# Order of ScalarE, VectorE and TensorE work inside a step: x's halves, weight splits, the spread and the division

## The chip, the cores and the metric

The kernel runs on one core of a Trainium2 chip. The metric is the device time of one execution in microseconds (us), the median of several runs. Lower is better. All arithmetic that matters for the error is float32: most products are made of three matmuls on "upper" and "lower" halves of each operand (a number rounded to fp32r, and what is left of it), so every operand needs two passes over it ahead of TensorE: one on ScalarE, which rounds (`..._upper`, `..._hi`), and one on DVE (VectorE), which subtracts (`..._lower`, `..._lo`).

## What is computed

Two layers of attention plus a mixture of experts on 4096 tokens of 512 numbers, cut here to its frame:

```python
x = L0_attn_x                                   # (2, 2048, 512)
xn = _layernorm(x)
s = _L0_attn_ref(xn, Wq, Wkv, Wk, Wv, Wo)       # 16 heads, window of 128 keys + 16 persistent ones
g = silu(_L0_ffn_ref(xn, ...))                  # 32 experts, 6 per token, and a shared one
x = x + s * g
xn = _layernorm(x)
s = _L1_attn_ref(xn, W_in, ...)                 # Y = (A * Q) @ W_out + X, A summed over the sequence
g = silu(_L1_ffn_ref(xn, router_weight, ...))
x = x + s * g
```

In the first attention each query tile sees its own 128 keys, the 128 before it, and the 16 persistent ones; softmax, times the values, then `Wo`.

## The kernel before, in words

The program is five phases, one after the other: `phase_front` (norm, projections, with the routing inside the next), `phase_attend` (first attention, L602), `phase_experts` (L1083), `phase_mix` (the combining stage, L1410) and `phase_last` (L2077). Each phase has one instruction stream for each engine, written out by hand and run in that order; semaphores tie the streams together. Nothing is reordered by a scheduler, so the order of the calls in a step is the order on the engine. An engine whose next instruction waits holds everything behind it.

**The attention stage** walks over 512 (tile, head) pairs in steps `s`, 16 a tile, 32 tiles. What each engine does in a step is a few calls. TensorE: `score(s + 3)` (L867, needs that DVE has read the score bank of three steps ago), `turn(s)` in odd steps (four transposes of a pair of heads' probabilities, L884), `values(u, g)` in every fourth (L897), in step 17 of a tile (`X_AT`) `turn_sums` (L907), then `spread` (L925: the inverse row sums of the tile, spread over the 32 columns of each head, out of `a_xT`) and `pers_values` (L913: the persistent keys' share, the last that is added to `a_psO`). DVE: `top(s + 3)` (L1027: mask, scale and row maximum), `copy_out` of transposed pairs (L1038), `divide` (L1051: `a_o` = `a_psO` times `a_rb`) and `out_lo`. ScalarE: `exps(s + 2)` (L972), `sums_out` (L988: writes `a_xT`), `inverse_out` (L994: writes `a_rb`), `out_hi` (L1000). `values(u + 1, 0)` overwrites `a_psO` and so waits for `divide(u)`.

**The combining stage** walks over 8 groups of 512 tokens, 18 steps `k` a group, with a shared expert of layer 0 in 6 blocks of three steps: gate product, up product, down product of the block before. `q` counts blocks. Next to it, the finished group is combined: `sums` (L1910, DVE: four additions out of `b_psY`), `gates` (L1787, ScalarE: four Silu), `residual` (L1918, L1920, L1922, DVE: three passes for each of four tiles), then the norm, and for each of its four tiles TensorE's `turn` (L1676, transposes into `c_psX`), `x_upper` (L1804, ScalarE) and `x_lower` (L1961, DVE), `router` (small matmuls into `c_psX`, waits for `x_lower`), and two products `keys(t, 0)` and `keys(t, 1)` into the one bank `c_psK`, which DVE empties after each (L1973). Those four tiles start at 8, 12, 16 and 20 steps behind the start of the group that follows, so the fourth falls into step 2 of the group after that, where the next group's `sums` and `gates` stand as well. The weights of block `q + 2` are split in the third step of each block: `gu_upper` (L1763, ScalarE) and `gu_lower` (L1883, DVE, waits for `gu_upper`). TensorE needs them four steps later.

In group 0 the stage also folds the norm's gamma and beta into layer 1's weights (`fold`, `fold_out`, `fold_upper`).

Of the kernel before, what the change touches and what calls it, by code (L numbers as in the profile page):

```python
# [601 lines left out]
def phase_attend(nc, env):  # L602
# [23 lines left out]
    with ctx:  # L626
# [137 lines left out]
        X_AT = 17  # L764
# [87 lines left out]
        def _(pe):  # L852
# [88 lines left out]
            for s in STEPS:  # L941
                if s + SR < N:
                    score(s + SR)
                if s < N:
                    turn(s)
                for g in range(NGR):
                    if (u := tile_of(s, GH * g + GH - 1 + LAG)) is not None:
                        values(u, g)
                if (u := tile_of(s, X_AT)) is not None:
                    turn_sums(u)  # L950
                if (u := tile_of(s, X_AT + 2)) is not None:
                    spread(u)
                if (u := tile_of(s, X_AT + 3)) is not None:
                    pers_values(u)
                for c in range(KC):
                    if (u := tile_of(s, X_AT + 8 + c)) is not None:
                        project(u, c)
# [59 lines left out]
        def _(dve):  # L1017
# [50 lines left out]
            for s in STEPS:  # L1068
                if s + SR < N:
                    top(s + SR)  # L1070
                if (u := tile_of(s, X_AT - 3)) is not None:
                    invert(u)
                if s < N:
                    copy_out(s)
                if (u := tile_of(s, X_AT + 4)) is not None:
                    divide(u)
                if (u := tile_of(s, X_AT + 5)) is not None:
                    out_lo(u)
                if (u := tile_of(s, X_AT + 12)) is not None:
                    finish(u)  # L1080
# [329 lines left out]
def phase_mix(nc, env):  # L1410
# [14 lines left out]
    with ctx:  # L1425
# [331 lines left out]
        def _(act):  # L1757
# [78 lines left out]
            for g, k, after in steps():  # L1836
                if g is not None:
# [8 lines left out]
                    elif q + 2 < QS:  # L1846
                        gu_upper(q + 2)
# [7 lines left out]
                for n, rel in after:  # L1855
# [12 lines left out]
                    if (t := tile_at(n, rel, XS)) is not None:  # L1868
                        x_upper(t)
                    if (t := tile_at(n, rel, XS + 4)) is not None:  # L1870
                        squares(t)
                    if rel == 25:
                        act.wait_ge(nn_ready, n + 1)
                        act.activation(rn[n % 2][:, :], nn[n % 2][:, :], ACT.Sqrt).then_inc(nroot_ready, 1)

        @block.vector
        def _(dve):
# [155 lines left out]
            for g, k, after in steps():  # L2033
                if g is not None:
# [6 lines left out]
                    elif k % 3 == 2:  # L2041
                        h_lower(q)
                        if q + 2 < QS:
                            gu_lower(q + 2)
                if g == 0:
                    fold(k)
                for n, rel in after:
# [11 lines left out]
                    if (t := tile_at(n, rel, XS)) is not None:  # L2059
                        x_lower(t)  # L2060
# [11 lines left out]
                    if rel == A_AT + 1:  # L2072
                        dve.wait_ge(a_full, n + 1)
                        dve.tensor_copy(env.aparts[:, n, :], psA).then_inc(a_used, 1)

# [549 lines left out]
```

## Time and profile before

| | us |
|---|---|
| median of 3 runs (lowest, highest) | 4580.51 (4570.82, 4585.73) |
| the profiled execution: time, span | 4576.1, 4574.2 |
| attention stage, 385 to 952: length, PE busy, DVE busy, ACT busy | 567, 496, 369, 385 |
| combining stage, 2460 to 3246: length, PE busy, DVE busy, ACT busy | 786, 729, 371, 249 |
| TensorE waits in the attention stage for `a_xT` (27 times) | 18.9 |
| TensorE waits in the attention stage for `a_o` (25 times) | 17.4 |
| TensorE waits in the combining stage for x's lower half (18 times) | 26.8 |
| TensorE waits once for the fold's first sum | 7.4 |

The first column names a thing, the second gives it in us of the one profiled execution (but for the median). TensorE (PE) is the busiest engine in both stages, at 87% and 93% of them.

### The profile page before, as it was taken

The numbers are of one execution on the slowest core, as the hardware profiler recorded it, in microseconds if no ns is written. First come the engines' busy times: TensorE is split into PE (matmuls) and PEld (weight loads), VectorE is DVE, ScalarE is ACT, GpSimd is POOL, SyncE is SP. The second block draws the span as 40 slices with busy tenths as digits, with TensorE's granted clock in tenths as the row PEclk, the third lists the DMA queues.
The fourth block names the chain that finished last, engine by engine and source line by source line (L and its number), as shares of the span: only waits on it lengthen the run. The fifth ranks groups of instructions, "written<-read, shape, count | busy, mean of one in ns | idle before, by whom it ended". The sixth has DMA issues, their size and how long they took to land. (4 is left out here: it accounts for less than half of the span.)

```text
span 4574.2 us, 68643 instructions
## 1 busy us (share of the span) xinstructions
PE 4213.9 (92%) x23045; PEld 3557.8 (78%) x23046; DVE 2097.7 (46%) x4006; ACT 1663.7 (36%) x3234; POOL 1220.5 (27%) x1809
## 2 busy tenths in 40 slices
PE   6966888879999999999997999998799999999998
PEld 5854667668989888888886777776578888788887
DVE  4457666644444444444444554453333333333333
ACT  2214766643343434343332333332222222222222
POOL 0012444434444444444442233333100000000000
PEclk8877999989999999999998999998899999999999
DMA  5776666635555556565554443342423222221221
GB/s 199 284 231 162 128 136 128 114 96 118 113 126 120 130 112 130 114 131 118 124 116 130 168 150 121 133 134 71 143 76 104 97 87 75 97 99 63 97 81 48
DMA packets 351750, 560.87 MB, mean 123 GB/s; under 512 B 33057, under 2 KB 198593, under 8 KB 347330
## 3 DMA queue, kind: packets, MB, share of 16 engines
q1 hardware_dynamic: 282770, 394.19, 29.3%
q0 software_dynamic: 68784, 164.10, 16.9%
q8 instruction: 120, 1.97, 0.2%
q14 instruction: 76, 0.62, 0.1%
HBM read 383.84 MB, written 174.34 MB: 122 GB/s over the span
## 5 line engine op out<-in xcount | busy, mean ns | idle before, releaser
L1206 POOL DMA_INDIRECT acc_d<-e_yw,e_to x208 | 336.1, 1616 | 342.4 <-ACT e_yw L1339 330.6
L2244 POOL DMA_DIRECT2D out<-d_res x32 | 17.3, 542 | 1305.3 <-DVE d_res L2476 1305.3
L2423 DVE TENSOR_TENSOR d_h<-d_sg,d_psU 128x512 f32<-128x512 f32 x144 | 99.1, 688 | 520.1 <-PE d_psU L107 461.7
L972 ACT ACTIVATE a_pr<-a_sm,a_nmax 128x272 f32<-128x272 f32 x512 | 264.0, 516 | 164.3 <-DVE a_nmax L1027 122.5
L105 PE MATMUL e_psG<-e_gu,e_xT 128*128 128x352 f32 x832 | 286.3, 344 | 8.5 <-DVE e_xT L1393 8.5
L1401 DVE TENSOR_TENSOR e_h<-e_sg,e_psU 128x352 f32<-128x352 f32 x208 | 108.4, 521 | 387.3 <-ACT e_sg L1352 383.9
L1027 DVE CUSTOM_DVE_ANT_0 a_sm<-a_psS,a_mask 128x272 f32<-128x272 f32 x512 | 213.1, 432 | 156.7 <-PE a_psS L867 134.8
L107 PE MATMUL e_psU<-e_gu,e_xT 128*128 128x352 f32 x832 | 268.8, 323 | 0.0
L105 PE MATMUL e_psU<-e_gu,e_xT 128*128 128x352 f32 x832 | 268.5, 323 | 0.0
L106 PE MATMUL e_psU<-e_gu,e_xT 128*128 128x352 f32 x832 | 268.3, 323 | 0.0
L106 PE MATMUL e_psG<-e_gu,e_xT 128*128 128x352 f32 x832 | 267.8, 322 | 0.0
L107 PE MATMUL e_psG<-e_gu,e_xT 128*128 128x352 f32 x832 | 267.8, 322 | 0.0
L105 PE MATMUL e_psY<-e_wd,e_hT 128*128 128x512 f32 (+1 forms) x624 | 264.0, 423 | 1.2 <-DVE e_hT L1384 1.2
L2351 ACT ACTIVATE d_hT<-d_h 128x512 fp32r<-128x512 f32 x144 | 91.0, 632 | 459.0 <-DVE d_h L2423 401.0
L1187 POOL DMA_INDIRECT e_xg<-xn_d,e_idx x208 | 208.4, 1002 | 177.1 <-POOL e_idx L1184 166.3
L1352 ACT ACTIVATE e_sg<-e_psG 128x352 f32<-128x352 f32 x208 | 96.8, 465 | 425.7 <-PE e_psU L107 424.7
L107 PE MATMUL e_psY<-e_wd,e_hT 128*128 128x512 f32 (+1 forms) x624 | 248.0, 397 | 0.0
L106 PE MATMUL e_psY<-e_wd,e_hT 128*128 128x512 f32 (+1 forms) x624 | 247.5, 397 | 0.0
L2345 ACT ACTIVATE d_sg<-d_psG 128x512 f32<-128x512 f32 x144 | 86.0, 598 | 422.9 <-PE d_psG L107 422.7
L1333 ACT ACTIVATE e_hT<-e_psH 128x384 fp32r<-128x384 f32 x208 | 102.7, 494 | 372.8 <-PE e_psY L107 200.0
L105 PE MATMUL d_psG<-d_x,d_gu 128*128 128x512 f32 x576 | 225.1, 391 | 12.9 <-DMA d_x<-xT_d 12.7
L105 PE MATMUL d_psU<-d_x,d_gu 128*128 128x512 f32 x576 | 227.5, 395 | 0.0
(423 smaller groups left out, 11901.8 us busy)
## 6 DMA issues: line engine op xcount, KB each, us to landing
d_gu_raw<-in_wgu SPq DMA_DIRECT2D x144, 512.0 KB, 3.2
qk_d<-f_qk SPq DMA_DIRECT2D x32, 1024.0 KB
a_q<-qk_d SPq DMA_DIRECT2D x96, 256.0 KB
a_k<-qk_d SPq DMA_DIRECT2D x96, 256.0 KB
e_rawgu<-in_w_gate SPq DMA_DIRECT2D x32, 704.0 KB
e_rawgu<-in_w_up SPq DMA_DIRECT2D x32, 704.0 KB
b_gu_raw<-in_wgu SPq DMA_DIRECT2D x40, 512.0 KB, 3.9
xT_d<-f_xT SPq DMA_DIRECT2D x16, 1024.0 KB
```

The costliest lines, as they stand in the source:

```text
L105: pe.matmul(out, lhs[0], rhs[1], start=first, stop=False, **kw)
L106: pe.matmul(out, lhs[1], rhs[0], start=False, stop=False, **kw)
L107: return pe.matmul(out, lhs[0], rhs[0], start=False, stop=last, **kw)
L972: act.activation(pr[half][:, h % HH, :], sm[s % SR][:, :], ACT.Exp, bias=nmax[s % SR][:, :], scale=-1.0, accum_out=rs[u % 2][:, h:h + 1]). ...
L1027: dve.tensor_tensor_reduce(out=sm[s % SR][:, :], in0=psS[s % SR][:, PERSIST:2 * KW], in1=m[:, :], scale=-SCALE, scalar=3.0e38, op0=ALU.add ...
L1187: pool.indirect_dma_start(xg[:, :], None, env.xn_d, bass.IndirectOffsetOnAxis(ap=idx[:, :].bitcast(U32), axis=0))\
L1206: pool.indirect_dma_start(env.acc_d, bass.IndirectOffsetOnAxis(ap=to[:, :].bitcast(U32), axis=0), yw[:, :], None, compute_op=ALU.add).then ...
L1333: act.activation(hT[0][:, :, :], psH[:, :, :], ACT.Copy).then_inc(hT_hi, 1)
L1352: act.activation(sg[:, :], psG[:, 0:M], ACT.Silu).then_inc(sg_ready, 1)
L1401: dve.tensor_tensor(hv[:, :], sg[:, :], psU[:, 0:M], ALU.mult).then_inc(h_ready, 1)
L2351: act.activation(h2[q % 2][0][:, :], hv[q % 2][:, :], ACT.Copy).then_inc(h_hi, 1)
L2423: ins = dve.tensor_tensor(hv[q % 2][:, :], sg[q % 2][:, :], psU[:, :], ALU.mult)
```

## The change

Four places are touched, two in each stage; no instruction is added or removed on any engine.

- TensorE, attention: `spread(u)` goes from the end of step 19 to step 20, behind that step's score and ahead of `values(u, 3)`.
- DVE, attention: `divide(u)` goes to the front of its step 21, ahead of `top` and `copy_out`.
- ScalarE and DVE, combining: `x_upper` and `x_lower` go ahead of the combining work of the step (and of the fold).
- ScalarE and DVE, combining: `gu_upper` and `gu_lower` go to the end of the step, behind the combining work (and the fold).

```diff
@@ phase_attend, tensor @@
+                if (u := tile_of(s, X_AT + 3)) is not None:
+                    spread(u)
                 for g in range(NGR):
...
-                if (u := tile_of(s, X_AT + 2)) is not None:
-                    spread(u)
@@ phase_attend, vector @@
             for s in STEPS:
+
+                if (u := tile_of(s, X_AT + 4)) is not None:
+                    divide(u)
                 if s + SR < N:
                     top(s + SR)
...
-                if (u := tile_of(s, X_AT + 4)) is not None:
-                    divide(u)
@@ phase_mix, scalar @@
-                    elif q + 2 < QS:
-                        gu_upper(q + 2)
+
+                for n, rel in after:
+                    if (t := tile_at(n, rel, XS)) is not None:
+                        x_upper(t)
...
-                    if (t := tile_at(n, rel, XS)) is not None:
-                        x_upper(t)
...
+                if g is not None and k % 3 == 2 and q + 2 < QS:
+                    gu_upper(q + 2)
@@ phase_mix, vector @@
-                        if q + 2 < QS:
-                            gu_lower(q + 2)
+                for n, rel in after:
+                    if (t := tile_at(n, rel, XS)) is not None:
+                        x_lower(t)
                 if g == 0:
                     fold(k)
...
-                    if (t := tile_at(n, rel, XS)) is not None:
-                        x_lower(t)
...
+                if g is not None and k % 3 == 2 and q + 2 < QS:
+                    gu_lower(q + 2)
```

DVE in the combining stage, step 2 and the two steps after it, of a group from the third on. Before (`c_xT` is x's lower half, `b_gu` the weights' split, `c_acc` the sums, `c_s` and `c_x` the residual):

```order
L1903 TENSOR_TENSOR b_hT<-b_h,b_hT 128x512
L1883 TENSOR_TENSOR b_gu<-b_gu_raw,b_gu 128x1024
L1910 TENSOR_TENSOR c_acc<-b_psY,c_acc 128x512 x4
L1961 TENSOR_TENSOR c_xT<-c_psX,c_xT 128x512
L1918 TENSOR_TENSOR c_s<-c_s,c_acc 128x512
L1920 TENSOR_TENSOR c_x<-c_s,c_x 128x512
L1922 BN_STATS c_st<-c_x 128x6
```

The same place now:

```order
L1906 TENSOR_TENSOR b_hT<-b_h,b_hT 128x512
L1964 TENSOR_TENSOR c_xT<-c_psX,c_xT 128x512
L1913 TENSOR_TENSOR c_acc<-b_psY,c_acc 128x512 x4
L1886 TENSOR_TENSOR b_gu<-b_gu_raw,b_gu 128x1024
L1921 TENSOR_TENSOR c_s<-c_s,c_acc 128x512
L1923 TENSOR_TENSOR c_x<-c_s,c_x 128x512
L1925 BN_STATS c_st<-c_x 128x6
```

The split has moved from ahead of the sums to between the sums and the residual, and x's lower half from behind the sums to ahead of them.

ScalarE at the same place. Before (`c_acc` is the four Silu of the gates, `c_sq` the squares, `b_sg` the Silu of the next block):

```order
L1782 ACTIVATE b_hT<-b_h 128x512
L1763 ACTIVATE b_gu<-b_gu_raw 128x1024
L1787 ACTIVATE c_acc<-c_acc 128x512 x4
L1804 ACTIVATE c_xT<-c_psX 128x512
L1813 ACTIVATE c_sq,c_n<-c_kv 128x512 x2
L1775 ACTIVATE b_sg<-b_psG 128x512
```

The same place now:

```order
L1783 ACTIVATE b_hT<-b_h 128x512
L1805 ACTIVATE c_xT<-c_psX 128x512
L1788 ACTIVATE c_acc<-c_acc 128x512 x4
L1814 ACTIVATE c_sq,c_n<-c_kv 128x512 x2
L1764 ACTIVATE b_gu<-b_gu_raw 128x1024
L1776 ACTIVATE b_sg<-b_psG 128x512
```

The split's upper half now stands behind the gates and the squares.

DVE in the attention stage, steps 20 to 22 of a tile, before (each pair of `ISA` rows is one `top`):

```order
L1027 ISA a_sm,a_nmax<-a_psS,a_mask 128x272
L1027 ISA a_nmax 128x1
L1027 ISA a_sm,a_nmax<-a_psS,a_mask 128x272
L1027 ISA a_nmax 128x1
L1038 COPY a_pT<-a_psP 128x512
L1051 TENSOR_TENSOR a_o<-a_psO,a_rb 128x512
L1027 ISA a_sm,a_nmax<-a_psS,a_mask 128x272
L1027 ISA a_nmax 128x1
L1055 TENSOR_TENSOR a_oT<-a_o,a_oT 128x512
```

And now:

```order
L1027 ISA a_sm,a_nmax<-a_psS,a_mask 128x272
L1027 ISA a_nmax 128x1
L1051 TENSOR_TENSOR a_o<-a_psO,a_rb 128x512
L1027 ISA a_sm,a_nmax<-a_psS,a_mask 128x272
L1027 ISA a_nmax 128x1
L1038 COPY a_pT<-a_psP 128x512
L1027 ISA a_sm,a_nmax<-a_psS,a_mask 128x272
L1027 ISA a_nmax 128x1
L1055 TENSOR_TENSOR a_oT<-a_o,a_oT 128x512
```

The division has moved ahead of one `top` and one copy.

## Rows read from the trace of the kernel before

**Rows 1.** Waits of TensorE, attention stage: engine, line, releaser: us, times, longest.

```profile
PE a_psXY L925 <- ACT a_xT L988: 18.9, 27, 1.6
```

**Rows 2.** Timeline, TensorE, one attention tile: start us, length us, instruction, idle before.

```profile
701.13 1.15 PE L925 MATMUL a_psXY<-a_xT,a_sel 16*128 16x128 f32 x8 [0.81 <-ACT a_xT L988]
...
702.21 0.40 PE L867 MATMUL a_psS<-a_k,a_q 96*128 96x288 f32 x1
...
703.11 1.16 PE L913 MATMUL a_psO<-a_xT,a_vp 128*128 128x128 f32 x8
...
706.39 0.65 PE L897 MATMUL a_psO<-a_pT,a_v 128*32 128x128 f32 x16 [0.70 <-DVE a_o L1051]
```

**Rows 3.** Timeline, DVE and ScalarE, the same tile.

```profile
699.91 0.44 DVE L1027 CUSTOM_DVE_ANT_0 a_sm<-a_psS,a_mask 128x272 f32<-128x272 f32 x1 [0.95 <-PE a_psS L867]
...
704.56 0.44 DVE L1027 CUSTOM_DVE_ANT_0 a_sm<-a_psS,a_mask 128x272 f32<-128x272 f32 x1 [1.35 <-PE a_psS L867]
...
705.56 0.68 DVE L1051 TENSOR_TENSOR a_o<-a_psO,a_rb 128x512 f32<-128x512 f32 x1
...
706.16 0.43 DVE L1027 CUSTOM_DVE_ANT_0 a_sm<-a_psS,a_mask 128x272 f32<-128x272 f32 x1
...
706.82 0.51 ACT L972 ACTIVATE a_pr<-a_sm,a_nmax 128x272 f32<-128x272 f32 x1
```

**Rows 4.** Timeline, DVE and TensorE, a tile of the other kind.

```profile
666.25 0.44 DVE L1027 CUSTOM_DVE_ANT_0 a_sm<-a_psS,a_mask 128x272 f32<-128x272 f32 x1 [1.53 <-PE a_psS L867]
...
666.80 1.15 PE L925 MATMUL a_psXY<-a_xT,a_sel 16*128 16x128 f32 x8 [0.72 <-ACT a_xT L988]
```

**Rows 5.** Timeline, TensorE, combining stage, group 5, steps 2 to 5.

```profile
2887.16 0.66 PE L1676 MATMUL c_psX<-ident,c_xn 128*128 128x128 f32 x4
...
2892.23 0.27 PE L105 MATMUL c_psX<-c_wr,c_xT 128*128 128x8 f32 x1 [1.65 <-DVE c_xT L1961]
...
2896.46 0.39 PE L105 MATMUL c_psK<-wkv,c_xT 128*128 128x512 f32 x1
...
2899.26 0.39 PE L105 MATMUL b_psY<-b_wd,b_hT 128*128 128x512 f32 x1
...
2902.21 0.50 PE L105 MATMUL c_psK<-wkv,c_xT 128*128 128x512 f32 x1
```

**Rows 6.** Timeline, DVE, the same steps.

```profile
2885.59 2.32 DVE L1883 TENSOR_TENSOR b_gu<-b_gu_raw,b_gu 128x1024 fp32r<-128x1024 f32 x1
2887.83 2.47 DVE L1910 TENSOR_TENSOR c_acc<-b_psY,c_acc 128x512 f32<-128x512 f32 x4
2891.48 0.69 DVE L1961 TENSOR_TENSOR c_xT<-c_psX,c_xT 128x512 fp32r<-128x512 f32 x1 [1.18 <-ACT c_xT L1804]
...
2901.42 0.73 DVE L1973 SCALAR_TENSOR_TENSOR c_kv<-c_psK,stat,bkv 128x512 f32<-128x512 f32 x1
...
2902.67 1.22 DVE L1883 TENSOR_TENSOR b_gu<-b_gu_raw,b_gu 128x1024 fp32r<-128x1024 f32 x1
```

**Rows 7.** Timeline, ScalarE, the same steps.

```profile
2888.54 2.43 ACT L1787 ACTIVATE c_acc<-c_acc 128x512 f32<-128x512 f32 x4 [4.66 <-DVE c_acc L1910]
2890.87 0.58 ACT L1804 ACTIVATE c_xT<-c_psX 128x512 fp32r<-128x512 f32 x1
...
2897.98 1.04 ACT L1763 ACTIVATE b_gu<-b_gu_raw 128x1024 fp32r<-128x1024 f32 x1
```

**Rows 8.** Timeline, TensorE, the same two instructions in group 2.

```profile
2616.86 0.66 PE L1676 MATMUL c_psX<-ident,c_xn 128*128 128x128 f32 x4
...
2634.84 0.50 PE L105 MATMUL c_psK<-wkv,c_xT 128*128 128x512 f32 x1
```

**Rows 9.** Timeline, TensorE, group 4: the up product behind the wait, and its successor.

```profile
2802.78 0.48 PE L105 MATMUL b_psU<-b_x,b_gu 128*128 128x512 f32 x1
...
2807.22 0.39 PE L105 MATMUL c_psK<-wkv,c_xT 128*128 128x512 f32 x1
```

**Rows 10.** Timeline, TensorE, step 9 of group 5: the router's wait.

```profile
2917.14 0.27 PE L105 MATMUL c_psX<-c_wr,c_xT 128*128 128x8 f32 x1 [0.46 <-DVE c_xT L1961]
```

## The prediction, made before the changed kernel was run

> **What bounds the kernel now.** I first read the busy time by stretches: TensorE fills both touched stages almost alone, so a microsecond counts only where TensorE waits. Next I read who waits for whom in each stage, and last the timelines around those waits. In the attention stage two waits come back in nearly every tile. The spread waits for `a_xT` (18.9 us over 27 tiles [rows 1]; 0.81 us in the tile shown [rows 2]), and `values` of the next tile waits 0.70 us for `a_o` [rows 2], in 25 of 32 tiles. In the combining stage, in each group from 2 to 7, the router's first matmul waits 1.65 us in step 3 for x's lower half [rows 5] and about 0.5 us in step 9 [rows 10]. The change aims at all four.
>
> The reader should look at one more thing in [rows 5, 6]. DVE's first emptying of `c_psK` ends at 2901.42 + 0.73 = 2902.15 by the row's own length, and TensorE begins `keys(t, 1)`, which needs that bank, at 2902.21. So in group 5 two limits lie on top of each other: TensorE's own work, and DVE's chain from `sums` to that emptying. Taking away the 1.65 us ahead of it gives nothing unless DVE's chain gets shorter as well. In this group TensorE ran at its full clock from step 2 to step 5.
>
> **Combining stage, steps 2 to 5 of groups 2 to 7.** I rebuild the chain of group 5 in the new order, from the `turn` at 2887.16, which ends at 2887.82 [rows 5].
> - ScalarE is free then (it sat idle 4.66 us ahead of the gates [rows 7]), so `x_upper` (0.58) ends about 2888.5, and `x_lower` may start. Its successor starts 0.6 us later, at 2889.1. The router is ready at about 2889.2, ahead of TensorE, which ends the gate product near 2890.4: the 1.65 us are gone.
> - `sums` run from 2889.1 to 2891.5 (2.47 us for four [rows 6]); they began at 2887.83 before. The last Silu starts when the last sum is there: 0.6 us (2.43 for four [rows 7]), to 2892.2. The two squares follow, some 1.3 us with the readings of their sums, to 2893.5. Only now comes `gu_upper`, 1.04 us [rows 7], to 2894.5.
> - DVE has nothing to do from 2891.5, but its next instruction is `gu_lower`, which waits for `gu_upper`. It runs from 2894.6 and takes 1.22 us (GpSimd's rotation, beside which it took 2.32 in this step before, is over by then; both lengths in [rows 6]). What is queued behind this wait: the residual of four tiles, the product of the next block, and the emptying of `c_psK`.
> - From the instruction behind `x_lower` (2892.09) to the emptying (2901.42) DVE took 9.3 us, 0.4 of it idle [rows 6]: 8.9. It starts at 2895.75, so the emptying begins at 2904.7 and `keys(t, 1)` at about 2905.4: 18.2 us behind the `turn`, where it was 15.05 [rows 5].
>
> TensorE is there at 2900 (from 2887.8 on, twelve matmuls of 512 columns each for the gate, up, key and down products at 2.80 us, which is 2896.46 to 2899.26 [rows 5], and 1.4 for the router). It then waits over 5 us, where it waited 1.65 before.
>
> The other groups differ in where they stood before: 17.98 us in group 2 [rows 8], and 16.5, 16.6, 15.05, 15.05 and 16.4 in groups 3 to 7 (the same pair of instructions). Together 97.6. In the new order each is bound by DVE and ScalarE, so all come to 18.2: 109.2. **Cost +11.6 us.** The spread of the old values is the clock: in groups 2, 3, 4 and 7 the up product behind the wait took 4.44 us instead of 2.80 [rows 9], the granted clock being at the lower of its two levels, and DVE was then the one that waited. In the new order such a stretch at that place is free, because DVE is later anyway.
>
> **What the longer wait does to the clock.** The trace shows stretches of ten or so matmuls at the lower clock (1.2 instead of 2.4 GHz) behind waits: each costs 4.44 - 2.80 = 1.64 us [rows 9]. After 1.65 us of waiting it came in four of six groups. After over 5 us I expect one in each, now in `keys(t, 1)` or the gate product, where nothing hides it: **+9.8 us**. The bounds are 0 and 19.7 (two such stretches per group). The Trainium skill (TensorE: Matmul & The Clock Gate, "What's actually happening") says that an array without work falls back to the lower clock and that activity gives it back. The trace agrees in kind, and that rule speaks against this change.
>
> **What is won elsewhere in this stage.** The 0.46 us in step 9 [rows 10] has `gu_upper` and `gu_lower` between TensorE's turn and x's halves; both move behind. Behind a slower step 5 TensorE also comes later there: 6 x 0.46 = **-2.8 us**. In group 0 the fold's first sum is bound by DVE; one split (1.22 us [rows 6]) no longer stands ahead of its last part, and TensorE waited 7.4 us for it. In group 1 the router's wait in step 9 gets shorter, while the norm's deviation comes later, because `gu_lower` now stands ahead of it and waits for the square root's engine. I take **-2 us** for both, bounds 0 and -4. In the two rounds behind the last group there are no splits, and DVE's chain (x's half, sums, residual) has the same sum in either order: 0. All other steps give the split three steps of cover (8 us and more), also where it now stands behind an emptying of `c_psK`: 0. SP's next weight load waits for the split, but has five steps, and the loads of `acc`, `s` and `x` queued behind it have the most of a group.
>
> Combining stage: 11.6 + 9.8 - 2.8 - 2 = **+16.6 us**, bounds 0 and +28.
>
> **Attention stage, the division.** `pers_values` ends at 703.11 + 1.16 = 704.27 [rows 2]. What it releases can start 0.15 us later (the division ended at 706.24, `values` began at 706.39 [rows 2, 3]): 704.42. DVE is idle then (1.35 us ahead of `top` at 704.56 [rows 3]). The division thus starts 1.1 us earlier, and the wait of 0.70 us for `a_o` disappears. But `top`, the copy and the next `top` come behind it: `top` at 705.0 instead of 704.56, and the following one at 704.42 + 0.60 + 1.00 = 706.02 instead of 706.16 (0.60 from the division to its successor, 1.00 from `top` over the copy to the division [rows 3]). TensorE's next transposes need the exponentials of that second `top`, which ran from 706.82 [rows 3]; they get 0.14 us from DVE and about as much again from `out_hi`, which leaves ScalarE earlier, but `exps` ahead of that comes 0.4 us later. I take 0.2 us a tile: 31 x 0.2 = **-6.2 us**. Bounds: 0, and 25 x 0.70 = -17.5. I stay near the lower end, since the row that ends last is the exponential and not the division.
>
> **Attention stage, the spread.** A score now goes ahead of it. In tiles as in [rows 2, 3] (13 of 31) the `top` that the score needs ends at 699.91 + 0.44 = 700.35, well ahead of the spread at 701.13, so the score (0.33 us from its start to the next instruction) fills the wait: 13 x 0.33 = -4.3. In most others [rows 4] that `top` ends at 666.69 and the spread could start at 666.80: the score has to wait for the same moment, and 0.05 us is left, -0.7 in all. **-5 us**, bounds 0 and -10. What the spread releases (`a_rb`) had half a microsecond of cover ahead of the division.
>
> Attention stage: **-11.2 us**, bounds 0 and -27.
>
> **The sum.** +16.6 - 11.2 = +5.4 us. Against the profiled execution's 4576.1 that is 4581.5. That execution lies 4.4 us (0.1%) under the median of the three runs shown; against the median it is 4586, and this is my forecast. A measurement of this kernel can tell about 0.3% (13.7 us) from no change, so my forecast reads as "no change".
>
> **The rivals.**
> - *The splits find their room* (faster). If the residual could go on without `gu_lower`, DVE's chain would be 8.9 us behind 2891.5: the emptying would end at 2901.2 and each group would have 14.0 us instead of 16.3, so 6 x 14.0 = 84 against 97.6, -13.6, with -4.8 from elsewhere and no long wait: -18.4, with the attention's -11.2 -30 us: 4551. For it: the waits named first do vanish. Against it: the engine's order, in which the split stands ahead of the residual and behind the gates. It decides at whether `gu_upper` ends before the sums do. Chance 0.10.
> - *The clock falls twice per long wait* (slower). Place: `keys(t, 1)` and the gate and up products behind it, in groups 2 to 7. Price: 6 x 1.64 = +9.8 more, net +15.2: 4596. It decides from five of the six groups on. For it: the wait grows from 1.65 to over 5 us, and group 2 already had a longer slow stretch than the rest. Chance 0.16. The Trainium skill (TensorE: Matmul & The Clock Gate, "Why this matters for your kernels") warns against such idle gaps between bursts of matmuls, and its rule points to this side.
> - *The attention gains nothing* (slower). The second `top` and its exponentials stay where they are because `exps` and `out_hi` change places on ScalarE: the 0.70 us turns into a wait for `a_pr` of the same length. Then +16.6: 4597. For it: the exponentials already end last. Chance 0.12.
>
> **How the numbers follow.** Forecast 0.62, rivals 0.10, 0.16 and 0.12. Faster by over 0.3%: 0.12 (the first rival, and a little of the forecast with the clock untouched and a larger gain of the division). Slower: 0.26 (the other two are at +0.33% and +0.36%, some of them fall just short, and some of the forecast's own tail is beyond). Within: 0.62. The range leaves out the first rival and a tenth beside: 4564 to 4604.
>
> **What would show it.** In the profile after: the router's wait of 1.65 us gone, and in its place a wait of some 5 us of `c_psK`'s second product for DVE, six times, some 30 us in all; DVE idle some 3 us ahead of the split in step 2, released by ScalarE's split; 18.2 us from turn to second key product. In the attention stage: the wait for `a_o` gone, that for `a_xT` smaller, and a new one of the transposes for `a_pr` behind it; the stage 11 us shorter, the combining stage some 17 longer. Wrong would be a second key product that starts less than 16 us behind the turn, or an attention stage that isn't shorter.

## The result, and the profile after

| | us |
|---|---|
| kernel before, median of 6 runs | 4580.98 |
| changed kernel, median of 6 runs (lowest, highest) | 4595.2 (4593.38, 4599.71) |
| ratio, 95% interval | 1.0043, 1.0032 to 1.0053 |

The change makes the kernel 0.43% slower. The time lies in the predicted range, 9 us above the forecast of 4586; of the verdicts it is "slower by over 0.3%", to which the prediction gave 0.26.

Where it went, by stretches of TensorE's timeline. The columns are: start and end, length, busy time (and count) of PE, PEld, DVE, ACT and POOL, TensorE's granted clock as a share of full speed, DMA share, GB/s. The kernel before, its attention stage (first score to the experts' first matmul) and its combining stage:

```profile
385.60:969.90 584.30, 497.09 (x4585) 391.04 (x4586) 375.28 (x1325) 388.85 (x1219) 241.38 (x392) 0.96 0.59 116
2460.00:3257.00 797.00, 729.32 (x3296) 581.50 (x3296) 371.81 (x641) 250.40 (x440) 251.54 (x306) 0.92 0.39 132
```

The changed kernel, the same two stages:

```profile
387.80:977.10 589.30, 509.99 (x4585) 400.01 (x4586) 371.90 (x1325) 386.05 (x1219) 242.01 (x392) 0.94 0.59 115
2463.10:3277.70 814.60, 722.59 (x3297) 576.44 (x3297) 362.10 (x641) 251.17 (x440) 253.47 (x306) 0.92 0.38 129
```

The combining stage is 17.4 us longer in these two traces (16.6 were forecast). This trace of the kernel before is at the long end: in four other traces whose combining stage is in the old order (e1, e3, e4 and e8 below) the stage takes 789.5 to 791.4 us, so the loss is 17 to 25. The attention stage is 5.0 us longer, where it was to be 11.2 shorter. TensorE's idle time in it (length less busy) did fall, from 87.2 to 79.3 us, but its busy time rose by 12.9 at a lower granted clock.

TensorE's waits in the changed kernel (us in total, times, longest) answer to [rows 1, 5]:

```profile
PE c_psK L105 <- DVE c_kv L1976: 40.4, 11, 6.9
PE a_psXY L925 <- ACT a_pr L972: 16.5, 31, 1.5
PE c_psX L105 <- DVE c_xT L1964: 15.9, 12, 3.7
PE a_psO L897 <- ACT a_pr L972: 7.1, 22, 0.4
```

The wait of `keys` for `c_kv` was 4.4 us in all before. The spread's wait for `a_xT` [rows 1] has become one for `a_pr`, nearly as long. The wait of `values` for `a_o`, 17.4 us before, is gone.

Group 5 in the new order (timeline of all engines, steps 2 to 5), against [rows 5 to 7]:

```profile
2896.11 0.66 PE L1677 MATMUL c_psX<-ident,c_xn 128*128 128x128 f32 x4
...
2898.76 2.42 ACT L1788 ACTIVATE c_acc<-c_acc 128x512 f32<-128x512 f32 x4 [1.36 <-DVE c_acc L1913]
...
2902.32 1.04 ACT L1764 ACTIVATE b_gu<-b_gu_raw 128x1024 fp32r<-128x1024 f32 x1
...
2903.40 1.23 DVE L1886 TENSOR_TENSOR b_gu<-b_gu_raw,b_gu 128x1024 fp32r<-128x1024 f32 x1 [2.88 <-ACT b_gu L1764]
...
2914.19 0.79 PE L105 MATMUL c_psK<-wkv,c_xT 128*128 128x512 f32 x1 [5.01 <-DVE c_kv L1976]
...
2931.63 0.27 PE L105 MATMUL c_psX<-c_wr,c_xT 128*128 128x8 f32 x1 [0.91 <-DVE c_xT L1964]
```

This is the chain as it was drawn: DVE stands still for 2.88 us ahead of its half of the split, because ScalarE makes its half only behind the four gates and the squares; the second key product comes 18.08 us behind the turn and TensorE has waited 5.01 us for it. The last line is step 9 of the group: the router's wait there is 0.91 us, where the prediction had it vanish.

### The profile page after: what moved, and what is told of

Read it like the earlier page. It is cut to its first block and busy times, and to the rows that moved or that the text cites. A ratio compares the mean times of both kernels' runs of the same rounds, so it can differ in the third digit from the quotient of the medians.

```text
span 4594.8 us, 68644 instructions
## 1 busy us (share of the span) xinstructions
PE 4219.3 (92%) x23045; PEld 3561.4 (78%) x23046; DVE 2084.5 (45%) x4006; ACT 1661.8 (36%) x3234; POOL 1224.3 (27%) x1809
## 5 line engine op out<-in xcount | busy, mean ns | idle before, releaser
L2248 POOL DMA_DIRECT2D out<-d_res x32 | 17.4, 543 | 1305.4 <-DVE d_res L2480 1305.4
## 6 DMA issues: line engine op xcount, KB each, us to landing
e_rawgu<-in_w_gate SPq DMA_DIRECT2D x32, 704.0 KB
e_rawgu<-in_w_up SPq DMA_DIRECT2D x32, 704.0 KB
```

## The experiments

All are edits of the kernel before. Each was run against that kernel on the same chip; times are given as a difference of medians, with the ratio and its 95% interval (an estimate of its own, not the quotient of the two medians). The level of both moves from one set of runs to the next: the median of the kernel before was 4582.55 for e1 to e4, 4572.93 for e5 to e8, 4587.14 for e9 to e11 and 4541.74 for e12.

Two tables carry the readings. First the combining stage: from the timeline of TensorE the `turn` in step 2 (A), the second key product behind it (B), and the turns in steps 8 (C) and 12 (D); means over groups 2 to 7 in us. "Sum" is A to D; the rest of a group, 37.1 us, is the same in every kernel. "Slow" is the time in us, in all six groups together, in which the granted clock was at the lower of its two levels; work done in it takes about twice as long.

| kernel | A to B | B to C | C to D | sum | slow | stage |
|---|---|---|---|---|---|---|
| before | 16.3 | 11.1 | 25.1 | 52.5 | 47.8 | 797.2 |
| e1, e3, e4, e8 (stage as before) | 16.0 to 16.7 | 11.0 to 11.1 | 24.3 to 25.1 | 52.0 to 52.5 | 44.4 to 47.8 | 789.5 to 791.4 |
| changed | 18.1 | 12.7 | 25.0 | 55.8 | 51.2 | 814.6 |
| e2 both edits | 18.1 | 12.7 | 25.0 | 55.8 | 51.2 | 813.1 |
| e5 split behind x | 15.7 | 12.0 | 23.6 | 51.3 | 34.1 | 782.3 |
| e6 ScalarE's split early | 15.1 | 11.1 | 28.6 | 54.8 | 58.0 | 807.4 |
| e7 splits last alone | 16.8 | 11.6 | 26.3 | 54.8 | 61.4 | 808.1 |
| e9 wait filled | 18.1 | 11.1 | 26.6 | 55.7 | 44.4 | 808.8 |
| e10 lower half later | 14.6 | 11.1 | 24.7 | 50.4 | 17.1 | 791.0 |
| e11 best of both | 15.7 | 12.4 | 23.6 | 51.7 | 41.0 | 788.8 |
| e12 late once a group | 14.0 | 11.1 | 23.8 | 48.9 | 23.9 | 767.9 |

The five traces in the old order show how far these numbers move by themselves: the sum by 0.5 us a group, the stage by 8 us. A stage of one trace is therefore to be read against 789 to 797.

Second the attention stage, TensorE's busy and idle time in it (from the stretches of each trace). Kernels in one line were run on the same chip.

| order | attention as before: busy, idle | with attention edits: busy, idle |
|---|---|---|
| first set | before 497.1, 87.2 | changed 510.0, 79.3 |
| e1 to e4 | e2 510.2, 87.5 | e1 526.9, 79.5; e3 515.7, 80.3; e4 517.7, 88.4 |
| e5 to e8 | e5 501.9, 84.3; e6 496.0, 86.5; e7 503.1, 85.7 | e8 510.6, 70.6 |
| e9 to e11 | e9 508.7, 90.1; e10 511.5, 88.2 | e11 512.1, 77.4 |

**e1, both attention edits alone.**

```diff
@@ phase_attend, tensor, between turn(s) and values @@
+                if (u := tile_of(s, X_AT + 3)) is not None:
+                    spread(u)
...
-                if (u := tile_of(s, X_AT + 2)) is not None:
-                    spread(u)
@@ phase_attend, vector @@
             for s in STEPS:
+                if (u := tile_of(s, X_AT + 4)) is not None:
+                    divide(u)
```

> Both attention edits, the combining stage as before. By the prediction's reading the attention stage becomes 11 us shorter (6.2 for the divisions, 5 for the spread) and the time is about 11 us below the kernel before. By the reading of the changed kernel's trace it becomes some 5 us longer, because the spread, now behind the step's turn, waits also for the exponentials of that step: then the time is 2 to 8 us above, TensorE waits for a_pr ahead of the spread some 30 times at 0.5 us each, and the wait of a_psO for a_o is gone.

Measured: +4.1 us, ratio 1.0003 (0.9990 to 1.0016). No gain; the 11 us of the prediction (0.24%) are outside the interval. The stretch and two waits of its trace:

```profile
388.00:994.40 606.40, 526.94 (x4584) 416.32 (x4585) 371.12 (x1325) 389.00 (x1219) 242.98 (x392) 0.91 0.56 112
```

```profile
PE a_psS L867 <- ACT a_xT L988: 14.5, 25, 1.2
PE a_psXY L925 <- ACT a_pr L972: 11.8, 31, 1.5
```

Idle time fell by 8 us against e2, which has the old order here, and busy time rose by 17.

**e2, both edits of the combining stage alone** (the diff of `phase_mix` above, without that of `phase_attend`).

> Both edits of the combining stage, the attention stage as before. The prediction's reading: the combining stage is 17 us longer (about 800 instead of 798 less the new waits: the stretch from the first d_psG matmul's predecessor b_psG is 797 us before, 814 after), the time 16 to 18 us above. If the whole loss of the changed kernel were the attention's and noise of its place, it would be within 5 us of the kernel before. Rows looked for: six waits of TensorE for c_kv above 4 us, DVE's wait of about 3 us for the split that ScalarE makes.

Measured: +18.8 us, ratio 1.0038 (1.0026 to 1.0049). The whole loss of the change is this stage's; its length, 813.1, is within 2 us of the changed kernel's. The wait of `c_psK` is there at 37.3 us:

```profile
PE c_psK L105 <- DVE c_kv L1974: 37.3, 11, 5.0
```

**e3, the division alone**, and **e4, the spread alone** (one half each of e1's diff).

> Only the divisions are moved to the head of DVE's step, the spread stays. Reading after the result: the spread's new wait costs, the earlier division gains 0.2 to 0.3 us in each of 31 tiles, so this alone is 6 to 10 us below the kernel before. Rival: the attention's loss comes from the division, which now stands ahead of the row maxima: top(s + 2) is then late, TensorE's wait for a_nmax grows from about 4 us to over 10, and the time is above.

> Only the spread is moved behind the step's turn, the division stays. Reading after the result: the wait for a_xT (27 of which about 10 us gone) gives way to one for a_pr of some 16 us in all, the values and the division come about 0.2 us later in each tile, and the time is 6 to 12 us above the kernel before. By the prediction's reading it is up to 5 us below.

Measured: e3 -1.6 us, 0.9997 (0.9984 to 1.0010); e4 +7.3 us, 1.0010 (0.9998 to 1.0023). On whole times neither is settled. TensorE's idle time tells them apart: e3 has 80.3 against e2's 87.5, so the division gives the 7 us (6.2 forecast); e4 has 88.4, so the spread gives nothing, where 5 were forecast. The expected wait for `a_pr` is in e4's trace, and in e3's it is not:

```profile
PE a_psS L867 <- ACT a_xT L988: 14.4, 29, 0.8
PE a_psO L897 <- DVE a_o L1051: 12.9, 19, 0.7
PE a_psXY L925 <- ACT a_pr L972: 9.0, 31, 1.5
```

The first row names ScalarE, since it ended last; in the code a score waits only for DVE's reading of its bank, and in the tile read that ends at the same moment (696.98, and `a_xT` at 697.03). So the wait of the spread for `a_xT`, 21.9 us in e2, has become 14.4 us ahead of the score and 9.0 us ahead of the spread. In e3 that same wait of the spread is 30.2 us instead of 21.9: part of what the earlier division wins in `values` is waited for again there.

**e5, the splits directly behind x's halves**, ahead of the combining work, on both engines.

```diff
@@ phase_mix, scalar; the same on vector with x_lower, gu_lower @@
+                for n, rel in after:
+                    if (t := tile_at(n, rel, XS)) is not None:
+                        x_upper(t)
+                if g is not None and k % 3 == 2 and q + 2 < QS:
+                    gu_upper(q + 2)
```

> Combining stage: x's halves first, and the two splits directly behind them, ahead of the combining work; attention as before. Reading after the first four runs: x first takes away the router's waits for c_xT (26.8 us before, 15.9 in the changed kernel) and costs nothing elsewhere, while the splits behind the combining work bring the 37 to 40 us of waits for c_kv. So here the wait for c_xT is about 16 us, that for c_kv under 8, TensorE's idle time in the stage 56 to 60 us (66 before) and the time 5 to 10 us below the kernel before. Rival: the split behind x's half is late enough for the key products that a wait for c_kv of 2 to 3 us per group stands again: then the time is 0 to 8 us above.

Measured: -7.8 us, ratio 0.9986 (0.9974 to 0.9998). The time is as expected. The mechanism is not: the wait for `c_kv` grew to 23.0 us and idle time in the stage was 69.4 us, not 56 to 60. B stands 15.7 us behind A, since DVE's split now runs between x's half and the sums. What was gained most is from C to D, 23.6 for 25.1, and TensorE's busy time:

```profile
2459.10:3241.40 782.30, 712.92 (x3297) 571.17 (x3297) 366.64 (x641) 251.34 (x440) 251.61 (x306) 0.93 0.40 135
```

Busy time is 712.9 instead of 729.3 for the same matmuls (722.5 to 725.3 in e1, e3, e4 and e8), so the low clock took fewer of them. Against those four the stage is 7 to 9 us shorter, which fits the 7.8 us; the 15 us to the kernel before's own trace do not.

**e6, ScalarE's half of the split early, DVE's half last.**

```diff
@@ phase_mix, scalar: x_upper directly behind the old place of gu_upper; vector as in the changed kernel @@
                     elif q + 2 < QS:
                         gu_upper(q + 2)
+                for n, rel in after:
+                    if (t := tile_at(n, rel, XS)) is not None:
+                        x_upper(t)
```

> As the changed kernel's combining stage, but ScalarE makes its half of the split ahead of its combining work as before, and only DVE's half stands last; attention as before. If the wait of c_psK comes from DVE's idle time of about 3 us for ScalarE's half, ahead of its own, the waits for c_kv fall from 37 us to about 20 and the time is 2 to 8 us above the kernel before. If it comes from DVE's own half of the split standing between the chain and the key products, they stay near 37 us and the time is 14 to 20 us above.

Measured: +13.4 us, ratio 1.0024 (1.0013 to 1.0034). The wait for `c_kv` is 19.4 us, as the first theory said, and A to B is 15.1 us, as in a group before without a slow stretch there. So DVE's wait for ScalarE is the whole 3.0 us against the changed kernel. DVE's own 1.22 us have taken the place of the 1.18 us that DVE stood idle for x's upper half before [rows 6]; e12 below, with neither, has 14.0. But the time is not what that theory said:

```profile
2891.19 1.22 DVE L1884 TENSOR_TENSOR b_gu<-b_gu_raw,b_gu 128x1024 fp32r<-128x1024 f32 x1
...
2901.98 0.50 PE L105 MATMUL c_psK<-wkv,c_xT 128*128 128x512 f32 x1 [2.05 <-DVE c_kv L1974]
...
2918.26 0.27 PE L105 MATMUL c_psX<-c_wr,c_xT 128*128 128x8 f32 x1 [1.84 <-DVE c_xT L1962]
```

The first row shows DVE's split without a wait. The last is the router in step 9: it waits 1.84 us, and C to D became 28.6 us. ScalarE's split stands ahead of `x_upper` there, as it did before (1.04 us [rows 7]), and ScalarE also comes to that step later than before, as in the changed kernel, where the wait is 0.91 us. The wait, which was 0.46 us before [rows 10], explains 1.4 of the 3.5 us; the rest goes with matmuls at the lower clock (58.0 us of it, the second most of all kernels).

**e7, the splits last, x's halves in their old place.** (The last two lines of e5's diff at the end of the step, nothing else.)

> Only the splits go last, x's halves stay where they were; attention as before. The waits for c_kv are those of the changed kernel (37 to 40 us), those for c_xT are those of the kernel before or smaller, since the split no longer stands ahead of x's half in step 2 (16 to 27 us). Time 14 to 24 us above the kernel before. If x's halves first were the cause, it would be within 5 us of it.

Measured: +12.2 us, ratio 1.0018 (1.0006 to 1.0031); a little under the range given. The wait for `c_kv` was 12.6 us, not 37 to 40, for two reasons: with x's half behind them the sums start at once, and DVE's emptying comes 1.3 us earlier than in e2 (B is 16.7 us behind A in five groups, 18.1 in e2); and TensorE comes later itself (24.9 us for `c_xT`). The stage is 808.1 us. The splits at the end of the step are what costs, with x's halves in either place.

**e8, both attention edits, but the spread ahead of the turn.**

```diff
@@ phase_attend, tensor @@
                     score(s + SR)
+                if (u := tile_of(s, X_AT + 3)) is not None:
+                    spread(u)
                 if s < N:
                     turn(s)
```

> Both attention edits, but the spread stands between the step's score and its turn, so that it does not wait for the exponentials of that step; combining as before. TensorE's wait for a_pr ahead of the spread is gone, its idle time in the attention stage falls from 79 us (both edits as in the changed kernel; 87 in the kernel before) to 65 to 72. If idle time is what decides, the time is 8 to 16 us below the kernel before. Rival: the clock gives the gain back, as in the first runs (TensorE's busy time in the stage 516 to 527 us with the edits, 497 and 510 without): then busy time grows by about what idle time falls, and the time is within 6 us of the kernel before.

Measured: -5.9 us, ratio 0.9984 (0.9973 to 0.9995). TensorE is idle for 70.6 us in the stage, 9 fewer than with the spread behind the turn and 14 to 16 fewer than in the three other kernels of that chip, whose attention stage is the old one; busy for 510.6, where those have 496 to 503. A spread in its new place waits 0.30 us for `a_xT`:

```profile
712.89 1.15 PE L925 MATMUL a_psXY<-a_xT,a_sel 16*128 16x128 f32 x8 [0.30 <-ACT a_xT L988]
```

The idle time went as the first theory said, but the time is at the edge of the rival's range (within 6 us): at least half of what was won came back as busy time.

**e9, the long wait filled.** As e2, but TensorE repeats seven of the down product's accumulations in step 5 ahead of its wait (each 0.70 us; a repeat starts the accumulation anew, so the sums are the same).

```diff
@@ phase_mix, tensor, down_of @@
-                for j in range(GT):
-                    if m == 0 and g:
+                for r in range(11 if m == 0 and g > 1 else GT):
+                    j = r % GT
+                    if m == 0 and g and r < GT:
...
-                              [wd[h][0:k, m, :] for h in range(2)], m == 0, m == NB - 1)
+                              [wd[h][0:k, m, :] for h in range(2)], m == 0,
+                              m == NB - 1 or (m == 0 and g > 1 and r < 7))
```

> As e2_combining_both, but TensorE repeats seven of the four-matmul... seven accumulations (three products of 512 columns per quarter, 0.70 us each, 84 matmul instructions... counted simply: seven times 0.70 us, 4.9 us) of the first block's down product in step 5 of groups 2 to 7; a repeat starts the accumulation anew and gives the same sums. It is work ahead of the 5.01 us wait for c_kv, so nothing the chain of DVE needs comes later. If the wait also costs 1.64 us of low clock behind it, six times, the time from the second key product to the next turn falls back from 12.6 to 11.1 us, the wait to under 0.3 us, and the time is 8 to 10 us BELOW e2_combining_both, although TensorE does 29 us more work. If the clock has no part in it, the time is that of e2_combining_both (0.38% above the kernel before) or 1 to 3 us above that.

Measured: +19.2 us against the kernel before, ratio 1.0046 (1.0032 to 1.0060), which cannot be told from e2's 1.0038. Group 5:

```profile
2918.71 0.50 PE L105 MATMUL c_psK<-wkv,c_xT 128*128 128x512 f32 x1 [0.26 <-DVE c_kv L1976]
...
2934.07 0.27 PE L105 MATMUL c_psX<-c_wr,c_xT 128*128 128x8 f32 x1 [0.90 <-DVE c_xT L1964]
...
2936.65 0.63 PE L105 MATMUL b_psU<-b_x,b_gu 128*128 128x512 f32 x1
```

The wait is 0.26 us, and behind it nothing is slow: B to C is 11.1 us. But slow matmuls (0.63 us instead of 0.39) now stand behind the 0.90 us wait of the router in step 9, in five of the six groups, and C to D grew from 25.0 to 26.6. The sum is 55.7 us, 55.8 in e2. Group 4, A to C and C to D, in e9 and then in e2:

```profile
2807.99:2837.13 29.14, 28.89 (x135) 23.67 (x134) 22.34 (x39) 12.49 (x20) 13.29 (x16) 1.00 0.57 211
2837.13:2863.52 26.39, 25.40 (x121) 21.03 (x120) 7.86 (x22) 8.26 (x15) 2.73 (x3) 0.87 0.22 78
```

```profile
2802.57:2833.16 30.59, 25.58 (x113) 20.81 (x113) 22.34 (x39) 12.48 (x20) 13.29 (x16) 0.94 0.55 204
2833.16:2857.95 24.79, 23.79 (x122) 20.01 (x121) 7.86 (x22) 8.26 (x15) 2.73 (x3) 0.93 0.23 80
```

So the slow stretch behind this wait comes from the wait, and work in its place takes it away, but the group pays for it elsewhere; why it comes back behind the next wait is not shown. B itself stands where DVE's chain puts it, filled or not, so the 29 us of added work (42 times 0.70) cost the groups nothing.

**e10, DVE's half of the split two steps later**, behind the emptying of `c_psK`; ScalarE as in e5.

```diff
@@ phase_mix, vector, end of the step @@
+                if g is not None and k % 3 == 1 and q and q + 1 < QS:
+                    gu_lower(q + 1)
```

> As e5_x_then_split on ScalarE; on DVE x's half first and the split's lower half two steps later, behind the emptying of c_psK, where nothing waits for it. DVE's chain in step 2 to 5 loses the split: turn to second key product falls from 15.7 (e5) to about 14 us in groups 2 to 7, that is 6 x 1.7 = 10 us, and in the first turn of each group's four the split no longer stands there either (18.0 to 18.7 us now). Time 12 to 20 us below the kernel before. Rival: the split two steps later collides with the next block's product or with the other emptying, and each group gets back less than 0.5 us: time 5 to 9 us below, as e5.

Measured: -1.7 us, ratio 0.9996 (0.9987 to 1.0005). A to B is 14.6 us, close to the 14 expected, and the groups are 5.7 us shorter in sum than e5's. Neither theory saw the loss: the weights of group 0 come too late, and the first turn starts 107.4 us into the stage instead of 93.6 (e5).

```profile
PE b_psG L105 <- DVE b_gu L1884: 43.8, 12, 18.1
```

In the kernel before, this wait is there once, 18 us at the stage's start; here eleven more hold 25.7 us, among them 1.1 us behind C in each of the six groups. The groups also show that a wait need not be followed by slow matmuls: B waits 1.5 us in all six, and B to C is 11.1 us each time.

**e11, e5 and e8 together.**

> e5_x_then_split and e8_spread_ahead_of_turn together, which touch different stages: 7.8 + 5.9 = about 14 us below the kernel before (10 to 17) if the stages are independent. If the clock gives part of it back in the stage that was not touched, 5 to 10.

Measured: -14.6 us, ratio 0.9968 (0.9956 to 0.9980). The two add up (7.8 + 5.9 = 13.7).

**e12, e11 with one split a group late**: that of step 2, from the third group on.

```diff
@@ phase_mix, vector @@
+                if g is not None and k % 3 == 2 and q + 2 < QS and (k > 2 or g < 2):
+                    gu_lower(q + 2)
+                if g is not None and g > 1 and k == 4:
+                    gu_lower(q + 1)
```

> As e11_best_of_both, but of the five splits a group only the one that fell into step 2 has its lower half two steps later, and only from the third group on; the others stay directly behind x's half. e10's trace gave 14.6 us from turn to second key product (15.7 in e5) and 24 steps' worth of turns in 520.5 us against 526.2, and lost 13.8 us ahead of the first turn, where TensorE waited for b_gu (2.31, 6.63, 1.92 and 7.26 us). Here the first is kept and the second is not there: 4 to 7 us below e11_best_of_both, that is 18 to 22 us (0.39 to 0.48%) below the kernel before. Rival: the interval gets shorter but a slow stretch behind it stays or moves, as in e9, so that the groups gain under 2 us: 13 to 16 us below the kernel before.

Measured: 4496.4 against 4541.74, -45.3 us, ratio 0.9905 (0.9888 to 0.9921), far more than either theory gave. The combining stage is part of it, in e12 and then in e11:

```profile
2411.30:3179.20 767.90, 710.57 (x3297) 569.47 (x3297) 363.64 (x641) 251.19 (x440) 245.81 (x306) 0.94 0.39 137
```

```profile
2462.70:3251.50 788.80, 718.88 (x3297) 575.22 (x3297) 366.78 (x641) 251.37 (x440) 251.96 (x306) 0.93 0.39 134
```

```profile
2833.18 0.50 PE L105 MATMUL c_psK<-wkv,c_xT 128*128 128x512 f32 x1 [0.90 <-DVE c_kv L1974]
```

The last row is e12's second key product in group 5: 13.97 us behind its turn, with 0.90 us of waiting, and B to C is 11.1 us, so no slow stretch follows there, nor in the other five groups. From A of group 2 to D of group 7 e12 takes 17 us less than e11, where 4 to 7 were expected: 1.7 us a group from DVE's chain (10.4), 1.4 a group from B to C (8.2), less 1.6 for one more slow stretch from C to D in group 5. Against the five traces in the old order this stage is 22 to 29 us shorter.

From C to D a slow stretch is left in every group of e12, and it stands behind no wait. Group 5, the whole of C to D and the rows in it:

```profile
2844.25:2869.41 25.16, 25.16 (x121) 21.28 (x120) 7.26 (x18) 6.26 (x11) 2.73 (x4) 0.86 0.41 154
```

```profile
2854.38 4.09 PE L1705 MATMUL c_psX<-c_rn,c_prod 128*128 128x1 f32 x32
2858.34 0.77 PE L105 MATMUL b_psY<-b_wd,b_hT 128*128 128x512 f32 x1
2858.91 0.63 PE L106 MATMUL b_psY<-b_wd,b_hT 128*128 128x512 f32 x1
```

TensorE is busy for all of the 25.16 us, and the granted clock falls behind 32 matmuls of one column each. The kernel before has a slow stretch at this place too, in all six groups.

Against e11's trace the rest of the difference lies in the attention stage, whose code is e11's. It took 536.8 us (589.5 in e11), at a granted clock of 0.98. One group of ScalarE's instructions stands out (busy us, mean ns, idle time ahead of it), in e12 and then in e11:

```profile
L988 ACT ACTIVATE a_xT<-a_psP 128x384 f32<-128x384 f32 x32 | 15.0, 469 | 2.9 <-PE a_psP L907 2.9
```

```profile
L988 ACT ACTIVATE a_xT<-a_psP 128x384 f32<-128x384 f32 x32 | 15.7, 491 | 43.0 <-remote 30.3 <-PE a_psP L907 12.7
```

In e12's run ScalarE goes on to `a_xT` at once; in every other trace it stands still for about 1 us ahead of it in most tiles (25.7 to 43.0 us in all), although TensorE's transposes ended earlier. The kernel before was faster in that set too (4541.74), so the level isn't the change's; whether the kernel before lacked the pause there is not known, since e12's is the only trace of that set. What it is stays open, and so does how much of the 45 us would be there under the conditions of the other runs: e11's 14.6 and the 17 of the groups make about 32. What A to B shows does not hang on it: the untouched intervals (18.4 and 18.7 us from D to the next A) are the same in both.

## Why the prediction was right or wrong

- **A to B, +11.6 us.** Measured 18.1 for 16.3, six times: +10.9. The chain held in each link: 18.08 us behind the turn (18.2), DVE idle 2.88 us (about 3), TensorE waiting 5.01 us (over 5). e6 shows its cause: with ScalarE's half early the interval is 15.1.
- **The clock, +9.8 us.** B to C grew by 1.3 to 2.1 us in the six groups, +9.8 in all, and e9 shows that these slow stretches come from the longer wait. The reading as a cost of the clock was only half right. Over the six groups the changed kernel has hardly more time at the lower clock: 51.2 us, 47.8 before. Before, five stretches stood in A to B, where they cost 7.3 us (97.6 less six times 15.05), and nine in C to D (24.3 us with one, 26.0 with two; 22.7 without any, in one group of e1 and one of e4). So of the 20.1 us that the six groups lost, the chain, 15.05 to 18.08, is 18.2, and what the clock took in B to C it mostly gave back in A to B.
- **Step 9, -2.8 us.** Wrong: C to D went from 25.1 to 25.0, -0.6 in all. The router's wait there is 0.91 us in group 5, where it was 0.46 [rows 10]. The split did leave its place ahead of x's halves, but ScalarE now comes to them later: DVE's residual and statistics of the group stand behind the split of step 2, ScalarE's norm waits 2.76 us for them (0.73 before), and `x_upper` starts 2.90 us behind the turn of step 8 (2927.35), where it was 1.83:

```profile
2925.46 1.52 ACT L1797 ACTIVATE c_xn<-c_x,stat 128x512 f32<-128x512 f32 x2 [2.76 <-DVE stat L1951]
...
2930.25 0.57 ACT L1805 ACTIVATE c_xT<-c_psX 128x512 fp32r<-128x512 f32 x1
```

- **Group 0 and the rest, -2 us.** 17.4 less the 20.1 of the six groups gives -2.7, but a stage that moves by 8 us between traces can't show a term of that size. That the stage loses is confirmed by e2, which has only these edits.
- **The division, -6.2 us.** Idle time -7 (e3), and the wait for `a_o` gone. The new wait was foreseen at the transposes; theirs for `a_pr` is the same (5.7 us, 5.9 before), and it is `values` that waits for `a_pr` (7.1 us, 1.1 before).
- **The spread, -5 us.** This is the step that failed. It said that a score now goes ahead of the spread, and the list of the change names nothing else. A `turn` goes ahead of it too, and in that even step a turn transposes nothing but still waits for the exponentials of its own step, which stand on ScalarE behind `a_xT`. In the changed kernel:

```profile
703.51 0.49 ACT L988 ACTIVATE a_xT<-a_psP 128x384 f32<-128x384 f32 x1 [1.04 <-PE a_psP L907]
703.90 0.51 ACT L972 ACTIVATE a_pr<-a_sm,a_nmax 128x272 f32<-128x272 f32 x1
...
704.55 1.15 PE L925 MATMUL a_psXY<-a_xT,a_sel 16*128 16x128 f32 x8 [0.80 <-ACT a_pr L972]
```

`a_xT` is ready at 704.0, the spread starts behind the exponentials at 704.55. e4 gives nothing for the move (88.4 us idle), and e8, which goes ahead of the turn as well, gets 9 us.
- **The attention as a whole, -11.2 us.** The stage is 589.3 us, 584.3 before, and "an attention stage that isn't shorter" was one of the two signs that the prediction named as proving it wrong. Even the 7 to 8 us of idle time that were won did not reach the time (e1: +4.1, within its interval of zero). The prediction counted idle time alone. In all four sets of runs the kernels with attention edits have more busy time than those without, by 1 to 17 us, and in three of the sets the granted clock is the same or lower (0.91 to 0.94, against 0.93 to 0.96). Six traces against seven, on a quantity that moves by 7 us between traces of the same order in one set, make this likely and no more; the mechanism was not isolated.
- **The range.** The time fell into 4564 to 4604 because the combining stage was read well and the range was wide enough for an attention stage that gives nothing. The forecast of "no change" was not met, and that the miss is only 9 us is in part luck: the attention stage alone was 16 us off in these traces.
- **The rivals.** "The attention gains nothing" (4597, chance 0.12) is the one that came, with the size of its time right (4595.2), but not by its mechanism: the division's gain was there. "The clock falls twice per wait" had the same time (4596) and did not happen: B to C grew by 1.3 to 2.1 us, which is one stretch of about 1.6 (in groups 2 and 5 the low clock lasted twice as long, but it began during the wait). "The splits find their room" did not come either, but its 14.0 us from turn to second key product is what e12 has (13.97), once DVE's half stands behind the residual and the emptying.

## What to carry to other kernels

An instruction that does nothing in a step can still wait in it: when a piece of work is moved, list the waits of all that it is moved behind, not their work. When the two halves of an operation sit on two engines, put the first where its engine is free and the second where nobody queues behind it; e12 does this, and it was the order of ScalarE's half, not DVE's own 1.2 us, that cost 3 us a group in the changed kernel. DVE's own half counts too where its chain is the limit: 1.7 us a group from e11 to e12. Judge such moves by the interval between two fixed rows of the limiting engine: where DVE's chain set it, it repeats to 0.1 us in the six groups (18.07 to 18.09), while whole times needed ten runs to show 0.1%. Where slow stretches fall into it, it does not (15.05 to 17.98 before), so look at the granted clock beside it.

## What the runs showed of the hardware

The time lost to the lower clock moved here from place to place more than it added up, and some orders had much less of it (47.8 us in the six groups before, 17.1 in e10, 23.9 in e12). In the combining stage each of the groups 2 to 7 of the kernel before holds two or three slow stretches, each worth 1.6 us. They stand at two kinds of places. One is behind a wait: of 1.65 us in step 3 and 0.56 us in step 9 before, of 2.66 us in e5, 5.01 us in e2, 0.90 us in e9. The other is behind the 32 matmuls of one column in C to D, where TensorE did not wait at all (e12). At one fixed place, the second key product, the rows of all kernels order themselves by the length of the wait ahead of it: none of 26 waits from 0.25 to 2.05 us (e6, e7, e9, e10, e12) was followed by a slow stretch, two of three waits of 2.31 us (e7), ten of twelve of 2.62 to 2.66 us (e5, e11), and all twelve of 5.01 us (changed, e2). In step 3 it came behind 1.65 us in four of six groups, so the length of the wait alone does not decide it.

Taking the longest wait away (e9) moved its stretch to the next wait. The Trainium skill (TensorE: Matmul & The Clock Gate, "Why this matters for your kernels") advises to leave no longer idle gaps between bursts of matmuls, since the array then falls to the lower clock. The rows agree at the gap itself: the stretch behind the 5.01 us came every time, and it went with the gap. They do not agree that closing the largest gap saves time: e9 closed it and won nothing.

The level of this kernel on one chip also moves by itself: 4572.93 for the kernel before in one set, 4541.74 in another on the same chip, with a 1 us pause of ScalarE per attention tile present in the traces of one and absent in the one trace (e12's) of the other. Only ratios to runs made beside it mean anything at 0.3%.
